# Turning Y block by block: sixteen copies from SBUF to SBUF per pair of tiles, in place of a store to DRAM and four loads

## The chip, the cores and the metric

One core of one Trainium2 chip runs the whole kernel. The metric is the device time of one execution in microseconds (us). The kernel before takes 1504.46 us, the median of three runs (1504.14 to 1504.58).

## What is computed

64 sequences (tiles) of 128 tokens with 512 channels pass one gated cross-attention layer and one gated feed-forward layer. Cut to what matters:

```python
x = x + tanh(g_xattn) * attention(layernorm(x), ctx)
#   attention: O = A V per head (A is one matrix per head, summed over the whole batch)
#   Y = (O - mean) / sqrt(var + eps) * gamma + beta       over the 512 channels of a token
#   out = (relu(xn @ wg) * Y) @ wo
x = x + tanh(g_ffn) * ffn(layernorm(x))
#   ffn: (silu(xn @ gate * gs) * (xn @ up * us)) @ down * ds,   512 -> 1408 -> 512
```

Every matrix product is made exact to about float32 by splitting operands in a high and a low part.

## The kernel before, in words

The 64 tiles are worked off in pairs, q = 0 to 31. The program of each of the five instruction streams is written out by hand, with semaphores between them. It has three stages. Up to about 380 us projections of all tiles are made and the relu gates W and the values V go to DRAM. From about 380 us to 1063 us the function `first_groups` runs eight groups of the feed-forward layer (each 11 steps of gate and up products and 4 steps of down products, 15 steps a group, four tiles each), and in the same steps the attention of pairs 2 to 31 is finished. After that six rounds do the feed-forward layer of the other 32 tiles with fewer products.

The attention of a pair is cut in pieces 0 to 12; `pieces(n)` lists for step n which piece of which pair is due. `first_step(q)` starts a new pair every 3.5 steps, in turns 3 and 4. A step is about 5 us, a pair about 20.7 us (620 us for thirty pairs). What each piece does for the turn of Y:

- Piece 1, ScalarE: `y_normal` writes the normalised tile, tokens on partitions, to `nbuf`.
- Piece 2, VectorE: `y_blocks` (line 1104) transposes each 32x32 block of both tiles in place of it, from `nbuf` to `tbuf` (in `misc`). The blocks are turned, but they do not yet stand where a full transpose would have them. For a tile from 6 on it first waits on `wys`, the store of the pair before, since `tbuf` is single.
- Piece 3, SyncE (SP): `y_out` stores `tbuf`, 512 KB, to `wy_scratch` in DRAM.
- Piece 4, SP: `y_in` waits for that store and for `wm` of the pair before (`wy_pair_mul`, line 1115, the last reader of `turned[0]`), and then loads through `blocks_in` (line 457) in four transfers of 128 KB, one for each 32 partitions of the target. They put the blocks in their places: channels on partitions.
- Piece 5, SP: `w_load` (line 364), 512 KB, the W of the same pair.
- Piece 6, ScalarE: `y_pair_affine` (line 713) waits for the four loads (`wyl`) and applies gamma and beta in place.
- Piece 7: `wy_pair_mul` on VectorE (needs the affine and W), `wy_pair_hi` on ScalarE (753), `wy_pair_lo` on GpSimd (1573); `x_again` on SP.
- Piece 9: `wo_pair` on TensorE (1803 and 1807); then x1 and its statistics on VectorE (1126 to 1132).
- Piece 12, SP: `x2_out` and `x1_store`. `x2_in` brings the normalised x1 back, turned in the same way by four loads, in steps 9 and 12 of a group.

All DMAs are issued by SP in one queue in the order of its program; a wait or a long issue holds all that stands behind it. TensorE works each step in one of two sets of PSUM banks: step n can start when VectorE has read step n-2 (`slot_free`; `hidden`, line 1267). The down products of steps 11 to 14 need the low parts that GpSimd makes (`hidden_lo`, line 1616) of all eleven hidden units; step 11 asks for the last one only near its end.

Of the kernel before, what the change touches and what calls it, by code (L numbers as in the profile page):

```python
# [52 lines left out]
def pieces(n):  # L53

    return [(q, n - first_step(q)) for q in range(2, B // 2) if 0 <= n - first_step(q) <= 12]
# [21 lines left out]
def gated_layer(nc, x, ctx_t, wh, wh_t, wg, wo, gate_t, up_t, down_t, cols, rows, decay, eye, out):  # L77
# [7 lines left out]
    with stack:  # L85
# [13 lines left out]
        def placed(name, shape, dt=f32):  # L99
            at[name] = -(-nc.sbuf_base // 32) * 32  # L100
            return sb(name, shape, dt)
# [12 lines left out]
        misc = placed("misc", [128, 1216])  # L114
        acc = misc[:, 0:512].rearrange("p (h n) -> p h n", h=4)
        stg = misc[:, 512:1216]
        tbuf = misc[:, 0:1024].rearrange("p (t n) -> p t n", t=2)
        wyt = [placed(f"wyt{i}", [128, 4, 256], f32r) for i in range(2)]
        turned = [placed(f"turned{i}", [128, 4, 256]) for i in range(2)]
        wh_first = [turned[0][:, 2 * i:2 * i + 2, :].rearrange("p k (h n) -> p (k h) n", h=2) for i in range(2)]  # L120
# [37 lines left out]
        nbuf = placed("nbuf", [128, 2, 512])  # L158
# [52 lines left out]
        wy_s = nc.dram_tensor("wy_scratch", [2, 128, D], f32, kind="Internal").ap()  # L211
# [90 lines left out]
        s = {name: stack.enter_context(nc.semaphore(f"s_{name}")) for name in SEMAPHORES}  # L302
# [4 lines left out]
        def _(e):  # L307
            p = Program(e, s)
# [34 lines left out]
            def v_load(q):  # L343
                if q:
                    p.wait_ge("vlo", q)
                else:
                    p.wait_ge("ctlo", ctl(NG - 1, 1))
                p.wait_ge("vst0", 16 * (q + 1))
                p.wait_ge("vst1", 16 * (q + 1))
                e.dma_start(raw[:, 0:2, :], v_s[:, 2 * q:2 * q + 2, :]).then_inc(s["vld"], 16)  # L350

            def w_load(q):
                if q == 0:
                    p.wait_ge("ctlo", ctl(NG - 1, 3))
                elif q == 1:
                    p.wait_ge("sst", 64)
                    p.wait_ge("sand", 16)
                elif q == 2:
                    p.wait_ge("tbwe", 2)
                else:  # L360
                    p.wait_ge("wylo", q - 2)
                p.wait_ge("wst0", 32 * (q // 2 + 1))
                p.wait_ge("wst1", 32 * (q // 2 + 1))
                e.dma_start(wt_of(q), w_s[q // 2, :, :, 256 * (q % 2):256 * (q % 2) + 256]).then_inc(s[f"wl{q % 2}"], 16)
# [12 lines left out]
            def x_again(q):  # L377
                if q >= 2:
                    p.wait_ge(f"x1s{q % 2}", 16 * (q // 2))
                else:  # L380
                    p.wait_ge("xn", 2 * q + 58)
                    if q:
                        p.wait_ge("ad", 1)
                e.dma_start(xr[:, 2 * (q % 2):2 * (q % 2) + 2, :], x_v[:, 2 * q:2 * q + 2, :]).then_inc(s[f"xa{q % 2}"], 16)

            def x1_store(q):
                p.wait_ge("x1", 2 * q + 2)
                e.dma_start(x1_s[:, 2 * q:2 * q + 2, :], xr[:, 2 * (q % 2):2 * (q % 2) + 2, :]).then_inc(s[f"x1s{q % 2}"], 16)

            def residual(q):  # L390
                p.wait_ge(f"x1s{q % 2}", 16 * (q // 2 + 1))
                if q >= 2:
                    p.wait_ge(f"out{q % 2}", 16 * (q // 2))
                else:
                    p.wait_ge("wolo", 4)
                    p.wait_ge("alo", 1)
                e.dma_start(xr[:, 4 + 2 * (q % 2):6 + 2 * (q % 2), :], x1_s[:, 2 * q:2 * q + 2, :]).then_inc(s[f"res{q % 2}"], 16)

            def out_store(q):
                p.wait_ge("of", 2 * q + 2)  # L400
                e.dma_start(out_v[:, 2 * q:2 * q + 2, :], xr[:, 4 + 2 * (q % 2):6 + 2 * (q % 2), :]).then_inc(s[f"out{q % 2}"], 16)

            def y_out(q):

                p.wait_ge("wyb", 2 * q - 2)
                if q > 2:
                    p.wait_ge("wyl", 64 * (q - 2))
                e.dma_start(wy_s.rearrange("t p n -> p t n"), tbuf).then_inc(s["wys"], 16)

            def x2_out(q):  # L410
                p.wait_ge("x2b", 2 * q - 2)
                e.dma_start(x2_s[q].rearrange("t p n -> p t n"), xbuf[:, :, :]).then_inc(s["x2s"], 16)
# [8 lines left out]
            def weights_copy(o, k):  # L421
                src, row = {G1: (gate_s, 0), G2: (gate_s, 256), U2: (up_s, 256)}[o]
                e.dma_start(ws_s[:, :, k, o, :].rearrange("j p n -> p j n"),
                            src[row + 128 * k:row + 128 * k + 128, :].rearrange("p (j n) -> p j n", n=128)).then_inc(s["gst"], 16)
# [27 lines left out]
            def blocks_in(scratch, dst, name):  # L452

                src = scratch.rearrange("t (u r) (c a j) -> a r c (t u) j", u=4, c=4, a=4)
                for a in range(4):
                    to = dst[32 * a:32 * a + 32, :, :].rearrange("r c (x j) -> r c x j", j=32)
                    e.dma_start(to, src[a]).then_inc(s[name], 16)

            def y_in(q):
                p.wait_ge("wys", 16 * (q - 1))  # L460
                p.wait_ge(*(("wm", q + 2) if q > 2 else ("wm", 4)))
                blocks_in(wy_s, turned[0], "wyl")

            def x2_in(q):
                p.wait_ge("x2s", 16 * (q - 1))
                if q > 2:
                    p.wait_ge("tb2e", q + 2)
                blocks_in(x2_s[q], turned[1], "x2l")
# [106 lines left out]
            for g in range(NS):  # L575
                for step in range(15):
                    if step == 0 and g:
                        out_store(2 * g - 1)
                    if step == 4:
                        residual(2 * g)  # L580
                        residual(2 * g + 1)
                    if 1 <= g <= 6 and step == 14:
                        weights_copy((G1, G2, U2)[(g - 1) // 2], (g - 1) % 2)
                    for q, piece in pieces(15 * g + step):
                        if piece == 12:
                            x2_out(q)
                            x1_store(q)
                        if piece == 3:
                            y_out(q)
                        if piece == 2 and 2 < q < B // 2 - 2:  # L590
                            v_load(q + 2)
                        if piece == 4:
                            y_in(q)
                        if piece == 5:
                            w_load(q)
                        if piece == 7:
                            x_again(q)
                    if g == 0 and step == 1:
                        x1_store(0)
                        x1_store(1)  # L600
                    if g == 0 and 2 <= step < 6:
                        down_load(step - 2)
                    if g + 1 < NS and step == (9 if g else 10):
                        x2_in(2 * g + 2)
                    if g + 1 < NS and step == (12 if g else 13):
                        x2_in(2 * g + 3)
                    if g == NS - 1:
                        if step == 5:
                            for q in range(4):
                                pair_in(2 * NS + q)  # L610
                        if step in (8, 9, 10):
                            weights_in(step - 8)
                    if step == 13:
                        out_store(2 * g)
# [3 lines left out]
            for m in range(NP):  # L618
                q = 2 * NS + 4 * m
                for j in range(NI):  # L620
                    n = NI * m + j
# [26 lines left out]
        def _(e):  # L648
            p = Program(e, s)
# [72 lines left out]
                affine(tile_of(turned[0], t), bank_y(t))  # L722

            def y_pair_affine(q):
                p.wait_ge("wyl", 64 * (q - 1))
                affine(turned[0], turned[0])

            def wy_hi(t):
# [139 lines left out]
            for g in range(1, NG):  # L868
                n, more = 4 * g + 4, g + 1 < NG
# [89 lines left out]
            for m in range(NP):  # L959
                for j in range(NI):  # L960
                    n = NI * m + j
# [19 lines left out]
        def _(e):  # L981
            p = Program(e, s)
# [114 lines left out]
            def y_blocks(t):  # L1097
                p.wait_ge("nr", t + 1)
                if t >= 6:
                    p.wait_ge("wys", 16 * (t // 2 - 2))  # L1100
                else:
                    p.wait_ge("alo", 1)
                    p.wait_ge("wolo", 4)
                e.transpose(tbuf[:, t % 2, :], nbuf[:, t % 2, :]).then_inc(s["wyb"])

            def wy_mul(t):
                p.wait_ge("aff", t + 1)
# [221 lines left out]
            for g in range(1, NG):  # L1329
                n, more = 4 * g + 4, g + 1 < NG  # L1330
# [117 lines left out]
            for g in range(NS):  # L1448
                for step in range(15):
# [15 lines left out]
                    for q, piece in pieces(15 * g + step):  # L1465
                        t = 2 * q
# [13 lines left out]
                    for q, piece in pieces(15 * g + step):  # L1480
                        t = 2 * q
# [7 lines left out]
            for m in range(NP):  # L1489
                t = 4 * NS + 8 * m  # L1490
# [3 lines left out]
                for j in range(NI):  # L1494
                    n = NI * m + j
# [646 lines left out]
```

## Time and profile before

| | |
|---|---|
| median of three runs | 1504.46 us |
| the profiled execution | 1504.5 us |
| its span, first to last instruction | 1502.7 us |
| TensorE busy in the span | 1482.3 us (99%) |
| VectorE, ScalarE, GpSimd busy | 1045.7, 679.0, 717.7 us |
| granted TensorE clock, mean of the span | 0.999 |
| mean busy share of 16 DMA engines by SP's queue | 67.4% |

The page gives each engine's busy time, the span in 40 slices, the DMA queues, the chain of work that ended last, and groups of instructions. PE is TensorE, PEld its weight loads, DVE VectorE, ACT ScalarE, POOL GpSimd, SP SyncE; "SPq L457" is a DMA issue at line 457. In a timeline a bracket gives how long the engine sat idle before the row and what ended that. SP has no compute work: its rows are issues, and their duration is the time for which the queue is held.

### The profile page before, as it was taken

The numbers are of one execution on the slowest core, as the hardware profiler recorded it, in microseconds if no ns is written. First come the engines' busy times: TensorE is split into PE (matmuls) and PEld (weight loads), VectorE is DVE, ScalarE is ACT, GpSimd is POOL, SyncE is SP. The second block draws the span as 40 slices with busy tenths as digits, with TensorE's granted clock in tenths as the row PEclk, the third lists the DMA queues.
The fourth block names the chain that finished last, engine by engine and source line by source line (L and its number), as shares of the span: only waits on it lengthen the run. The fifth ranks groups of instructions, "written<-read, shape, count | busy, mean of one in ns | idle before, by whom it ended". The sixth has DMA issues, their size and how long they took to land.

```text
span 1502.7 us, 20433 instructions
## 1 busy us (share of the span) xinstructions
PE 1482.3 (99%) x7226; PEld 1057.6 (70%) x7226; DVE 1045.7 (70%) x1516; ACT 679.0 (45%) x1067; POOL 717.7 (48%) x767
## 2 busy tenths in 40 slices
PE   7999999999999999999999999999999999999998
PEld 5888888888667777677677767666566666666665
DVE  7777778788657676767677676554767768768662
ACT  4444434445564545445354544534344344343442
POOL 5556666771444535435354544534137238137236
PEclk9999999999999999999999999999999999999999
DMA  6888888876688686777877787676383473572332
GB/s 231 295 267 272 267 273 281 260 223 227 209 247 242 175 255 206 206 243 210 228 233 204 224 220 234 181 222 158 101 223 114 117 216 114 138 211 95 130 109 85
DMA packets 374952, 306.09 MB, mean 204 GB/s; under 512 B 258560, under 2 KB 284672, under 8 KB 374656
## 3 DMA queue, kind: packets, MB, share of 16 engines
q1 hardware_dynamic: 374848, 304.74, 67.4%
q8 instruction: 60, 0.98, 0.3%
q14 instruction: 44, 0.36, 0.1%
HBM read 200.36 MB, written 117.31 MB: 211 GB/s over the span
## 4 chain that ended last, share of the span: by engine, by line
PE 87%; DVE 5%; POOL 3%; issue 2%; ACT 2%; DMA 1%; SPq 0%; DVEq 0%; POOLq 0%; ACTq 0%
PE ps L1815 15%; PE ps L1813 14%; PE pyb L1698 8%; PE ps L1733 5%; PE po L1698 5%; PE ps L1822 4%; PE ps L1820 4%; PE po L1815 4%; PE po L1813 4%; PE pyb L1803 3%; PE ptb L1803 3%; PE pyb L1822 3%; PE ptb L1822 3%; PE ptb L1820 3%; PE pyb L1820 3%; PE pyb L1807 2%
## 5 line engine op out<-in xcount | busy, mean ns | idle before, releaser
L1616 POOL TENSOR_TENSOR hid_low<-tmp,reg 128x512 f16<-128x512 f32 x88 | 118.7, 1349 | 132.4 <-ACT reg L764 132.4
L1698 PE MATMUL pyb<-reg,xreg 128*128 128x512 f32 x708 | 177.1, 397 | 2.0 <-DVE reg L1003 1.7
L1596 POOL TENSOR_TENSOR p5b<-p5b,p1b 128x512 f32<-128x512 f32 x44 | 56.5, 1283 | 215.5 <-ACT p5b L788 215.5
L1607 POOL TENSOR_TENSOR hsp<-hall,hsp 128x640 f16<-128x640 f32 (+2 forms) x72 | 136.3, 1909 | 33.2 <-ACT hsp L815 32.1
L1698 PEld LDWEIGHTS pyb<-reg,xreg 128*128 128x128 f32 x708 | 129.2, 188 | 28.6 <-DVE reg L1003 2.1
L834 ACT ACTIVATE tmp<-ps,colsb 128x512 f32<-128x512 f32 x88 | 60.5, 687 | 161.1 <-PE ps L1815 81.4
L1267 DVE SCALAR_TENSOR_TENSOR tmp<-ps,colsb,tmp 128x512 f32<-128x512 f32 x88 | 65.6, 746 | 78.2 <-PE ps L1813 43.0
L1573 POOL TENSOR_TENSOR wyt<-raw,wyt 128x1024 fp32r<-128x1024 f32 x30 | 73.8, 2461 | 83.6 <-ACT wyt L753 83.6
L1522 POOL TENSOR_SCALAR rs<-mv 128x1 f32<-128x1 f32 (+1 forms) x98 | 42.7, 436 | 138.8 <-DVE mv L991 106.7
L1815 PE MATMUL ps<-op,wbuf 128*128 128x512 f32 x352 | 103.9, 417 | 0.0
L1815 PE MATMUL ps<-reg,gate 128*128 128x512 f32 x352 | 103.3, 415 | 0.0
L1733 PE MATMUL ps<-reg 128*128 128x256 f32 x768 | 101.5, 285 | 0.8 <-DVE misc L1021 0.3
L1733 PEld LDWEIGHTS ps<-reg 128*128 128x128 f32 x768 | 97.1, 191 | 5.1 <-POOL reg L1569 1.4
L1527 POOL TENSOR_TENSOR rs<-rs,nhalf 128x1 f32<-128x1 f32 (+1 forms) x132 | 90.0, 682 | 11.0
L1815 PE MATMUL ps<-reg,up 128*128 128x512 f32 x352 | 91.9, 393 | 0.0
L1813 PE MATMUL ps<-op,wbuf 128*128 128x512 f16 x352 | 90.8, 380 | 0.3 <-issue 0.3
L1822 PE MATMUL ps<-xreg,reg 128*128 128x512 f32 x352 | 90.2, 403 | 0.8 <-POOL hid_low L1616 0.6
L1813 PE MATMUL ps<-x_low,gate 128*128 128x512 f16 x352 | 90.8, 380 | 0.0
L1234 DVE TENSOR_TENSOR nbuf<-po,p1b 128x512 f32<-128x512 f32 x44 | 30.4, 692 | 86.8 <-PE po L1813 43.6
L1813 PE MATMUL ps<-x_low,up 128*128 128x512 f16 x352 | 88.7, 380 | 0.8 <-DVE tmp L1267 0.7
L681 ACT ACTIVATE tmp<-pyb 128x512 f32<-128x512 f32 x59 | 35.3, 598 | 114.7 <-PE pyb L1698 114.6
L1569 POOL TENSOR_TENSOR reg<-raw,reg 128x512 fp32r<-128x512 f32 x62 | 83.2, 1341 | 5.0
(180 smaller groups left out, 3363.5 us busy)
## 6 DMA issues: line engine op xcount, KB each, us to landing
wbuf<-ws_scratch SPq DMA_DIRECT2D x44, 896.0 KB, 4.8
xr<-in_x SPq DMA_DIRECT2D x62, 512.0 KB, 5.6
raw<-in_ctx_t SPq DMA_DIRECT2D x32, 512.0 KB, 4.6
w_scratch<-tmp SPq DMA_DIRECT2D x64, 256.0 KB, 5.0
v_scratch<-tmp SPq DMA_DIRECT2D x64, 256.0 KB, 4.0
raw<-v_scratch SPq DMA_DIRECT2D x32, 512.0 KB, 6.7
x_scratch<-xr SPq DMA_DIRECT2D x32, 512.0 KB, 4.5
xr<-x_scratch SPq DMA_DIRECT2D x32, 512.0 KB, 5.9
```

The lines of the kernel that those rows point to most:

```text
L1527: e.tensor_tensor(dst, dst, nhalf[:, 0:dst.shape[-1]], ALU.pow).then_inc(s[name])
L1569: e.tensor_tensor(lo, raw[:, h, :], f(hi), ALU.subtract).then_inc(s["ctlo"])
L1573: e.tensor_tensor(wyt[1][:, :, :], wt_of(q), f(wyt[0][:, :, :]), ALU.subtract).then_inc(s["wylo"])
L1607: e.tensor_tensor(hsp[t % 2][1][:, i0:i1, :], hall[:, i0:i1, 128 * i:128 * i + 128], f(hsp[t % 2][0][:, i0:i1, :]), ALU.subtract).then_inc ...
L1616: e.tensor_tensor(hid[1][:, m % 11, :], tmp[:, m % 3, :], f(hid[0][:, m % 11, :]), ALU.subtract).then_inc(s["hlo"])
L1698: last = e.matmul(dst, lhs[a], rhs[b], start=(k == 0 and i == 0), stop=(k == n - 1 and i == 2))
L1733: last = e.matmul(ps[t % 2][:, h, :, :], ct[g % 2][i][:, h, 128 * b:128 * b + 128], wh_and_z(q, h, b), start=(n == 0), stop=(n == 2))
L1803: e.matmul(py(t), wyt_of(t)[0][:, k, :], wos[i][k], start=(k == 0 and i == 0), stop=False)
L1813: return e.matmul(dst, upper(wt), act[1], start=start, stop=stop, skip_group_check=True)
L1815: return e.matmul(dst, a, b, start=start, stop=stop, skip_group_check=True)
L1820: return e.matmul(dst, act, packed, start=start, stop=stop)
L1822: return e.matmul(dst, a, b, start=start, stop=stop)
```

## The change

`y_out` and `y_in` go, and `y_turn` stands at piece 4. It waits for the blocks (`wyb`) and for `wm` of the pair before, and issues sixteen transfers from `tbuf` straight to `turned[0]`: for each group a of 32 target partitions and each group u of 32 source partitions one transfer of 32 partitions x 8 blocks x 128 bytes, 32 KB. The semaphore `wyl` counts 256 for a pair. VectorE's `y_blocks` writes `tbuf` in another order within the partition (channel block outside, tile inside) and waits for the turn of the pair before (`wyl`), where it waited for that pair's store. The turn of x1 by way of DRAM stays as it is.

```diff
-        tbuf = misc[:, 0:1024].rearrange("p (t n) -> p t n", t=2)
+        tbuf = misc[:, 0:1024]
@@
-            def y_out(q):
+            def y_turn(q):
                 p.wait_ge("wyb", 2 * q - 2)
-                if q > 2:
-                    p.wait_ge("wyl", 64 * (q - 2))
-                e.dma_start(wy_s.rearrange("t p n -> p t n"), tbuf).then_inc(s["wys"], 16)
+                p.wait_ge(*(("wm", q + 2) if q > 2 else ("wm", 4)))
+                for a in range(4):
+                    to = turned[0][32 * a:32 * a + 32, :, :].rearrange("r c (t u j) -> r (c t) u j", u=4, j=32)
+                    for u in range(4):
+                        blocks = tbuf[32 * u:32 * u + 32, :].rearrange("r (x a j) -> r a x j", a=4, j=32)
+                        e.dma_start(to[:, :, u, :], blocks[:, a, :, :]).then_inc(s["wyl"], 16)
@@
-            def y_in(q):
-                p.wait_ge("wys", 16 * (q - 1))
-                p.wait_ge(*(("wm", q + 2) if q > 2 else ("wm", 4)))
-                blocks_in(wy_s, turned[0], "wyl")
@@
-                        if piece == 3:
-                            y_out(q)
...
                         if piece == 4:
-                            y_in(q)
+                            y_turn(q)
@@
             def y_pair_affine(q):
-                p.wait_ge("wyl", 64 * (q - 1))
+                p.wait_ge("wyl", 256 * (q - 1))
@@
             def y_blocks(t):
                 p.wait_ge("nr", t + 1)
                 if t >= 6:
-                    p.wait_ge("wys", 16 * (t // 2 - 2))
+                    p.wait_ge("wyl", 256 * (t // 2 - 2))
...
-                e.transpose(tbuf[:, t % 2, :], nbuf[:, t % 2, :]).then_inc(s["wyb"])
+                e.transpose(tbuf.rearrange("p (c t n) -> p c t n", c=4, t=2)[:, :, t % 2, :], nbuf[:, t % 2, :].rearrange("p (c n) -> p c n", c=4)).then_inc(s["wyb"])
```

## Rows read from the trace of the kernel before

**Rows 1.** The page: busy time, and the chain that ended last.
```profile
PE 1482.3 (99%) x7226; PEld 1057.6 (70%) x7226; DVE 1045.7 (70%) x1516; ACT 679.0 (45%) x1067; POOL 717.7 (48%) x767
PE 87%; DVE 5%; POOL 3%; issue 2%; ACT 2%; DMA 1%; SPq 0%; DVEq 0%; POOLq 0%; ACTq 0%
```

**Rows 2.** One stretch: length; PE, PEld, DVE, ACT, POOL busy; clock; DMA share.
```profile
380.00:1065.00 685.00, 681.75 (x3192) 474.08 (x3191) 452.40 (x661) 336.78 (x503) 306.42 (x360) 1.00 0.75 214
```

**Rows 3.** Waits of PE, 380 to 1065 us: total, times, longest.
```profile
PE ps L1820 <- POOL hid_low L1616: 0.6, 1, 0.6
...
PE pyb L1807 <- POOL wyt L1573: 0.2, 1, 0.2
```

**Rows 4.** Issues by source line: duration ns min/median/max; time to landing.
```profile
L457 SPq DMA_DIRECT2D turned<-wy_scratch x120: 557/674/2597, 390.8 to 986.2; - x120
...
DMA to landing us min/median/max: 2.6/3.3/7.9
...
L408 SPq DMA_DIRECT2D wy_scratch<-misc x30: 359/420/1222, 387.9 to 977.3; - x30
...
L364 SPq DMA_DIRECT2D raw<-w_scratch x31: 572/787/2092, 345.2 to 990.3; - x31
```

**Rows 5.** Timeline of SP, pairs 8 and 13: start, duration, line, transfer.
```profile
510.28 3.09 SPq L457 DMA_DIRECT2D turned<-wy_scratch  x4
513.42 0.66 SPq L412 DMA_DIRECT2D x_scratch<-xbuf  x1
...
514.70 0.79 SPq L364 DMA_DIRECT2D raw<-w_scratch  x1
...
608.92 3.15 SPq L457 DMA_DIRECT2D turned<-wy_scratch  x4
```

**Rows 6.** Timelines of DVE and ACT after pairs 8 and 13.
```profile
517.14 1.38 DVE L1104 STREAM_TRANSPOSE misc<-nbuf 128x512 f32<-128x512 f32 x2 [1.65 <-ACT nbuf L707]
521.37 2.07 ACT L713 ACTIVATE turned<-turned,colsb 128x256 f32<-128x256 f32 x4
523.47 1.23 DVE L1115 TENSOR_TENSOR raw<-raw,turned 128x1024 f32<-128x1024 f32 x1 [0.95 <-ACT turned L713]
...
619.41 1.29 DVE L1104 STREAM_TRANSPOSE misc<-nbuf 128x512 f32<-128x512 f32 x2
```

**Rows 7.** A hidden unit on DVE, and PE's next step in its banks.
```profile
500.56 0.75 DVE L1267 SCALAR_TENSOR_TENSOR tmp<-ps,colsb,tmp 128x512 f32<-128x512 f32 x1 [1.29 <-PE ps L1815]
...
505.29 1.04 PE L1813 MATMUL ps<-x_low,up 128*128 128x512 f16 x4
```

**Rows 8.** The chain that ended last, 405 to 432 us: start, length, what.
```profile
406.87 0.57 SPq L457
...
408.22 2.60 SPq L457
...
410.86 0.68 SPq L457
...
412.81 7.35 DMA raw<-w_scratch
...
428.76 1.19 PE pyb L1807 x4
```

**Rows 9.** Step 11 of the second group, 526 to 531 us.
```profile
526.80 0.75 DVE L1267 SCALAR_TENSOR_TENSOR tmp<-ps,colsb,tmp 128x512 f32<-128x512 f32 x1 [0.48 <-PE ps L1815]
...
529.52 1.27 POOL L1616 TENSOR_TENSOR hid_low<-tmp,reg 128x512 f16<-128x512 f32 x1 [3.69 <-ACT reg L764]
...
530.85 0.10 PEld L1820 LDWEIGHTS ps<-down_first,hid_low 128*128 128x128 f16 x1 [0.21 <-POOL hid_low L1616]
```

**Rows 10.** Waits of SP, 390 to 1010 us: total, times, longest.
```profile
SPq L40 <- DVE raw L1115: 163.1, 24, 13.6
...
SPq L457 <- DMA wy_scratch<-misc: 29.7, 11, 5.0
```

**Rows 11.** The page, W's load: count, KB each, median us to landing.
```profile
raw<-w_scratch SPq DMA_DIRECT2D x31, 512.0 KB, 6.2
```

## The prediction

> **What bounds the kernel now.** I read the page first: TensorE is busy for 1482.3 of 1502.7 us and the chain that ended last is 87% TensorE [rows 1]. The turn of Y takes place between 380 and 1065 us only, so I cut that stretch out: TensorE is busy in 681.75 of 685.00 us, idle for 3.25 us, at a granted clock of 1.00, the level of 2.4 GHz [rows 2]. This is the most that any relief of DMA, SP, VectorE or ScalarE can give back there; it is 0.22% of the time, and 0.2% (3.0 us) is about what a measurement of this kernel can tell from no change. The waits of TensorE in the stretch name no part of the turn directly; the nearest is 0.2 us for GpSimd's low part of W*Y, and the longest wait for the low part of a hidden unit is 0.6 us [rows 3]. So the question is not what is saved but whether the new order of SP's queue pushes something into TensorE's way. The DMA engines are busy for 0.75 of the stretch [rows 2], and SP often sits waiting: 163.1 us in 24 waits for the multiplication of the pair before, and 29.7 us in 11 waits for Y's own store [rows 10]. Of VectorE I need how late it may be: a hidden unit read by 501.31 (500.56 + 0.75) is asked for by TensorE at 505.29, a slack of 3.98 us [rows 7]. It is the tightest kind among the steady steps: there VectorE reads as soon as TensorE is done.
>
> **What is removed.** One store of 512 KB for each of thirty pairs: 0.42 us of SP's queue [rows 4], and the eleven waits of SP for it (29.7 us, [rows 10]). None of this is on TensorE's path: the loads start mostly when the multiplication of the pair before ends, not when the store lands. Credit: 0, at most the 3.25 us of idle TensorE.
>
> **What is added: issues.** Four issues of 128 KB become sixteen of 32 KB. The four take 557 ns at the least and 674 ns in the median each [rows 4], and 3.09 us together at pair 8 [rows 5]. No row shows a copy of 32 partitions x 8 runs from SBUF to SBUF. The store of Y (256 runs too, on 128 partitions) held SP for 359 ns at least, 420 in the median; W's load, with 512 runs, 572 [rows 4]. From one issue's end to the next start about 0.04 us pass (513.37 to 513.42 in [rows 5]). So a pitch of 0.40 us is the lower end (0.36 + 0.04) and 0.72 (0.674 + 0.04) the upper, if the count of runs should not matter at all. I take 0.45 (0.42 + 0.03, rounded), because 256 runs are what the store has. Sixteen are then 7.2 us (6.4 to 11.5) where four took 3.1. The bytes and the runs of 128 B are the same 4096 for a pair, so I cost the movement itself at no more than now and hidden below the issues. The last transfer should land some 2.3 us after its issue: the loads of 128 KB have a minimum of 2.6 and a median of 3.3 [rows 4], and these are a quarter of the size. From first issue to all landed: 15 x 0.45 + 2.3 = 9.0 us (8.2 to 14.1), where pair 8 has about 3.09 + 2.6 = 5.7 now.
>
> The Trainium skill speaks against this (DMA: Bandwidth & Descriptors, Rules for kernel authors: coalesce small transfers, below 64 KB one pays mostly overhead). Rows 5 show that overheads of neighbouring issues overlap here, four starting within 3.09 us though one lands 3.3 us after its issue [rows 4, 5]; if by the rule each of sixteen paid such a 2 us alone, a pair would need some 32 us, longer than the pair's 20.7, and the stage would be SP-bound.
>
> **What is added: a wait on VectorE.** `y_blocks` of the next pair waits until the turn has landed. At pair 8 the turn can start at 510.28 [rows 5] and the next blocks start at 517.14 [rows 6]: 6.86 us; every fourth pair from 8 to 28 is of this kind, by the list of pieces. 9.0 - 6.86 = 2.1 us of new wait there. Pair 13 stands for the roomy ones (608.92 to 619.41, 10.5 us) [rows 5, 6]; the rest lie between, so 0 to 2. Queued behind it are x1 with its statistics and the next hidden unit. The slack of 3.98 us [rows 7] hides 2.1. It costs something only where it falls ahead of step 11 of a group. Y's affine starts at 521.37 [rows 6], 11.09 us after the turn's start: 9.0 fits.
>
> **What is moved.** All behind the turn in SP's queue starts later by 7.2 - 3.1 = 4.1 us: x2_out, x1_store and w_load at pair 8. W's load is issued at 514.70 [rows 5]; at 518.8 plus a landing of 6.2 [rows 11] it is there at 525.0, and the multiplication that started at 523.47 [rows 6] is 1.5 us late. In most pairs the slack of this load hides the 4.1 us; pairs of the kind of 8 can lose 1 to 3 us on VectorE, again within 3.98.
>
> **Where it reaches TensorE.** Two places have no slack.
> (a) Pair 3, 406 to 429 us. The chain that ended last runs here through the four Y loads (406.87 to 411.54, 4.67 us, of which one issue stood for 2.60 us), W's load at 412.81 (7.35 us), and by way of GpSimd's low part to TensorE at 428.76 [rows 8]. The turn starts at the same moment (after the multiplication of pair 2) and holds the queue for 7.2 in place of 4.67 us: +2.5 us (1.8 to 6.8), all on the path. If the 2.60 us stand comes on top, it is 4.5.
> (b) Step 11 of the second group, right behind pair 8. The multiplication is 1.5 us late, so the hidden unit at 526.80 is about 1.5 late, and its low part at 529.52 too; TensorE already waited 0.21 us for it at 530.85 [rows 9]. +1.2 us. The 2.1 us of new wait ahead of the unit before it adds about 0.3.
> Sum: 2.5 + 1.2 + 0.3 = 4.0 us. In the other groups the multiplication of a pair of this kind falls two or more steps away from step 11, by the list of pieces, and TensorE's longest wait for a low part is 0.6 us [rows 3]; I take 0 for them.
>
> VectorE's transposes write four runs of 128 elements in place of one of 512; I cost this at nothing, up to 0.1 us each (60 of them, hidden by VectorE's idle third).
>
> **The sum.** 1504.5 us of the profiled execution (span 1502.7 and 1.8 around it; the median of the runs is 1504.46, the same) + 4.0 = 1508.5 us.
>
> **Rivals.**
> 1. Everything is absorbed. VectorE, ScalarE and SP idle enough, and at pair 3 the backlog of DMA is smaller because two stores are gone (the 2.60 us stand shows such a backlog [rows 8]), so that W lands when it did. For it: 3.25 us of idle TensorE in 685 [rows 2] show how forgiving the schedule is. Against it: the chain of rows 8 has not a microsecond of slack. Time 1504.5 (1503.5 to 1507). Chance 0.35.
> 2. Faster, the other side: the store and its traffic were behind part of the 3.25 us idle, and nothing new is late. It decides from the point where sixteen issues take no longer than the four plus the store, a pitch of 0.22 us, or where the queue's backlog ends sooner by more than the 2.5 us. At best 1501.3. Rows 4 hold no issue below 0.36. Chance 0.04.
> 3. The issue is dearer: a pitch of 0.6 to 0.72 us, since the four-issue rows stay at 0.67 however long the queue is free. The turn then needs 11 to 14 us, y_blocks waits 4.5 to 7 us in most pairs, which is over the slack of 3.98, and W comes 6.5 to 8.4 us late. At 0.72 some thirteen pairs lose 2.5 us on TensorE and pair 3 6.8: 1504.5 + 32 + 7 = 1543; at 0.6 mostly the ends of the groups and pair 3, about +15: 1520. Chance 0.13.
> 4. The page's rule, sixteen overheads one after another: 32 us for a pair instead of 20.7 gives 30 x 11.3 = +340 us. Chance 0.01.
>
> **How the numbers follow.** The forecast (1508.5, own range 1505.5 to 1513) has 0.47; about a sixth of it lies below 1507.5. Faster by over 0.2% 0.04; within 0.2% 0.35 + 0.08 = 0.43; slower 0.39 + 0.13 + 0.01 = 0.53. The range reaches down to 1503.8 for rival 1 and up to 1519 for the cheap end of rival 3: some 0.16 is left out.
>
> **What would show it.** Right: the turn's issues at about 0.41 us each, all sixteen within 7 to 7.5 us and landed in 9; a new wait of the transposes in `y_blocks` on a DMA into `turned`, about 2 us, 10 to 20 times, 30 to 45 us in total, with TensorE hardly idle; TensorE idle by 2 to 3 us more near 429 us behind GpSimd's `wyt`, and by about 1 near 531 us behind `hid_low`. SP's waits for the store gone. Wrong: if issues take 0.6 us or more (rival 3), if the transfers from SBUF land much later than 2.3 us after issue although the issues are short (ports or engines shared by both sides), or if TensorE's idle time in 380 to 1065 us stays at 3 us (rivals 1 and 2).

## The result and the profile after

The changed kernel takes 1598.66 us, the median of four runs (1596.0 to 1600.09), where the kernel before takes 1504.52 beside it: ratio 1.0626, 95% interval 1.0614 to 1.0639, so 94 us slower. The forecast said slower, by 4 us, within 1505.5 to 1513. The profiled execution spans 1596.7 us against 1502.7, 94.0 more.

The page of the changed kernel, the parts that answer rows 1, and the stretch of the turn (columns as in rows 2). The stage ends about 95 us later now, so a second stretch reaches to 1165 us:

```profile
PE 1509.0 (95%) x7226; PEld 1068.6 (67%) x7226; DVE 1045.9 (66%) x1516; ACT 679.8 (43%) x1067; POOL 715.2 (45%) x767
...
PE 50%; SPq 21%; DVE 12%; DMA 7%; issue 5%; ACT 3%; POOL 3%; DVEq 0%; ACTq 0%; POOLq 0%
SPq L411 17%; PE pyb L1694 8%; PE ps L1811 6%; PE ps L1809 6%; PE ps L1729 5%; PE po L1811 4%; PE po L1809 4%; DVE raw L1111 3%; PE pyb L1818 3%; PE ptb L1818 3%; PE ptb L1816 2%; PE pyb L1816 2%; PE po L1694 2%; DMA raw<-w_scratch 2%; DMA 
```
```profile
380.00:1065.00 685.00, 621.05 (x2817) 427.64 (x2816) 398.53 (x592) 304.17 (x456) 275.03 (x333) 0.97 0.59 168
380.00:1165.00 785.00, 713.46 (x3214) 486.87 (x3213) 456.69 (x668) 339.73 (x507) 306.01 (x361) 0.97 0.59 168
```

Every compute engine has the same work as before. But the chain that ended last, once 87% TensorE with nothing for SP's queue [rows 1], is half TensorE now, and 17% of it is line 411, the sixteen issues. TensorE was idle for 3.25 us of the stretch [rows 2]; now it is idle for 64 of 685. It is also busy for 26.7 us longer in all (1509.0 - 1482.3) with the same number of instructions, and the granted clock is 0.97 where it was 1.00. The other two stages have not changed. So of the 94 us, some 67 are new idle time of TensorE (94.0 - 26.7) and 27 are slower matmuls. TensorE waits for several engines; these are its two longest waits from 380 to 1165 us (total, times, longest), the first for VectorE to read a hidden unit, the second for the high part of W*Y:

```profile
PE ps L1809 <- DVE tmp L1263: 24.1, 12, 6.3
...
PE pyb L1799 <- ACT wyt L749: 15.4, 9, 4.1
```

The issues of the turn (columns as in rows 4) and who waited for them (us, times):

```profile
L411 SPq DMA_DIRECT2D turned<-misc x480: 585/611/2691, 387.6 to 1087.0; - x160
...
  DVE misc L1100: 163.7, 26
  ACT turned L709: 28.8, 11
...
DMA to landing us min/median/max: 1.9/1.9/6.4
```

An issue takes 611 ns, not 420. The turn spans 699.4 us from its first issue to its last (387.6 to 1087.0), where it spanned 595.4 [rows 4]: 104 us more, of which 8 are the longer last turn itself. The other 95 or so are 3.3 us for each of the 29 steps from pair to pair, so the loss is spread over the whole stage and not at a few places.

What a pair looks like, SP's timeline of the changed kernel (columns as in rows 5), pairs 9 to 11:

```profile
547.85 11.23 SPq L411 DMA_DIRECT2D turned<-misc  x16
559.12 0.60 SPq L415 DMA_DIRECT2D x_scratch<-xbuf  x1
559.76 0.47 SPq L388 DMA_DIRECT2D x_scratch<-xr  x1
560.27 0.85 SPq L364 DMA_DIRECT2D raw<-w_scratch  x1
...
576.07 10.91 SPq L411 DMA_DIRECT2D turned<-misc  x16
...
589.17 1.15 SPq L364 DMA_DIRECT2D raw<-w_scratch  x1
...
596.88 10.40 SPq L411 DMA_DIRECT2D turned<-misc  x16
```

An undisturbed turn, as that of pair 11, holds the queue for 10.40 us, and its last transfer lands 1.3 us after that, at 11.7 (the medians of the thirty turns are 10.79 and 12.17). Pair 8 shows how the delay comes back to its own start. These are rows of the chain that ended last between 495 and 553 us (start, length, what), from W's load for pair 6 to TensorE:

```profile
495.39 6.43 DMA raw<-w_scratch
501.92 2.05 DVE raw L1111
513.82 1.90 DMA turned<-misc
...
526.22 2.29 DVE raw L1111
538.37 1.89 DMA turned<-misc
540.99 0.67 DVE misc L1100
...
546.96 1.24 POOL hid_low L1612
548.34 4.61 PE ps L1818 x10
```

and VectorE, ScalarE and TensorE in the same stretch (in a timeline a bracket gives the idle time ahead of a row and what ended it):

```profile
540.35 1.31 DVE L1100 STREAM_TRANSPOSE misc<-nbuf 128x512 f32<-128x512 f32 x2 [6.54 <-DMA turned<-misc]
...
545.38 1.22 DVE L1111 TENSOR_TENSOR raw<-raw,turned 128x1024 f32<-128x1024 f32 x1
...
560.49 1.31 DVE L1100 STREAM_TRANSPOSE misc<-nbuf 128x512 f32<-128x512 f32 x2 [2.87 <-DMA turned<-misc]
...
574.82 1.18 DVE L1111 TENSOR_TENSOR raw<-raw,turned 128x1024 f32<-128x1024 f32 x1
...
560.42 2.08 ACT L709 ACTIVATE turned<-turned,colsb 128x256 f32<-128x256 f32 x4 [0.95 <-DMA turned<-misc]
...
548.34 4.61 PE L1818 MATMUL ps<-xreg,reg 128*128 128x512 f32 x10 [4.34 <-POOL hid_low L1612]
```

The multiplication of pair 7 ends at 528.51 (526.22 + 2.29). Only then may pair 8's turn start, and its last transfer lands at 540.3 (538.37 + 1.89). `y_blocks` of pair 9 has waited 6.54 us for that and starts at 540.35. Behind it on VectorE stand x1, the statistics, a hidden unit, and the multiplication of pair 8 (545.38 to 546.60). Only then may pair 9's turn start; it starts at 547.85, because SP is at other issues until 547.75. That is a loop: turn, landing, next pair's `y_blocks`, this pair's multiplication, next turn. It is tight in most pairs: `y_blocks` waits for the landing 26 times, and 25 of 29 turns start within 0.1 us of the end of the multiplication. The first round took 18.1 us (528.51 to 546.60), the next, in which more stands between `y_blocks` (560.49) and the multiplication (done at 576.00), 29.4. In the kernel before the same two rounds took 14.5 and 27.1 us (the multiplications end at 510.21, 524.70 and 551.77). The mean is now some 24 us a pair, where the period was 20.7.

### The profile page after: what moved, and what is told of

Same layout as the page of the kernel before. It is cut to its first block, busy times and chain, and to the rows that moved or that the text cites. A ratio compares the mean times of both kernels' runs of the same rounds, so it can differ in the third digit from the quotient of the medians.

```text
span 1596.7 us, 20734 instructions
## 1 busy us (share of the span) xinstructions
PE 1509.0 (95%) x7226; PEld 1068.6 (67%) x7226; DVE 1045.9 (66%) x1516; ACT 679.8 (43%) x1067; POOL 715.2 (45%) x767
## 4 chain that ended last, share of the span: by engine, by line
PE 50%; SPq 21%; DVE 12%; DMA 7%; issue 5%; ACT 3%; POOL 3%; DVEq 0%; ACTq 0%; POOLq 0%
SPq L411 17%; PE pyb L1694 8%; PE ps L1811 6%; PE ps L1809 6%; PE ps L1729 5%; PE po L1811 4%; PE po L1809 4%; DVE raw L1111 3%; PE pyb L1818 3%; PE ptb L1818 3%; PE ptb L1816 2%; PE pyb L1816 2%; PE po L1694 2%; DMA raw<-w_scratch 2%; DMA turned<-misc 2%
## 5 line engine op out<-in xcount | busy, mean ns | idle before, releaser
L1612 POOL TENSOR_TENSOR hid_low<-tmp,reg 128x512 f16<-128x512 f32 x88 | 113.6, 1292 | 109.7 <-ACT reg L760 109.7
L1100 DVE STREAM_TRANSPOSE misc<-nbuf 128x512 f32<-128x512 f32 x60 | 39.3, 692 | 166.3 <-DMA turned<-misc 163.7
L1520 POOL TENSOR_SCALAR rs<-mv 128x2 f32<-128x2 f32 (+1 forms) x34 | 8.2, 240 | 256.2 <-DVE mv L1128 256.1
L1818 PE MATMUL ps<-xreg,reg 128*128 128x512 f32 x352 | 96.3, 422 | 15.3 <-DVE tmp L1270 7.8
L760 ACT CAST reg<-tmp 128x512 fp32r<-128x512 f32 x88 | 54.1, 615 | 114.2 <-DVE tmp L1263 114.2
L1809 PE MATMUL ps<-x_low,gate 128*128 128x512 f16 x352 | 94.4, 392 | 1.5 <-DVE tmp L1263 1.5
L1818 PEld LDWEIGHTS ps<-xreg,reg 128*128 128x128 f32 x352 | 69.3, 199 | 34.1 <-DVE tmp L1270 8.9
```

The source lines that it names most:

```text
L1612: e.tensor_tensor(hid[1][:, m % 11, :], tmp[:, m % 3, :], f(hid[0][:, m % 11, :]), ALU.subtract).then_inc(s["hlo"])
L1809: return e.matmul(dst, upper(wt), act[1], start=start, stop=stop, skip_group_check=True)
L1818: return e.matmul(dst, a, b, start=start, stop=stop)
```

## The experiments

I name four theories. A: the loop just described, through the wait of `y_blocks`. B: SP's queue is held, whoever waits. C: transfers from SBUF to SBUF are slow in themselves, or disturb others. D: there are two loops, A's and a second through W's load, which stands behind the sixteen issues and which the multiplication needs before the next turn may start; both must be broken. Each kernel is the changed one with the edit shown, unless the text says otherwise.

**Four transfers in place of sixteen, from SBUF to SBUF.** 128 KB each. The blocks don't go to their places, since the source is read in another pattern.

```diff
-                    for u in range(4):
-                        ... e.dma_start(to[:, :, u, :], blocks[:, a, :, :])
+                    runs = misc[32 * a:32 * a + 32, :].rearrange("r (x j) -> r x j", j=38)
+                    e.dma_start(to, runs[:, :, 0:32]).then_inc(s["wyl"], 16)
```

> The changed kernel with four transfers of 128 KB from SBUF to SBUF a pair, each of 32 partitions x 32 runs of 128 bytes, from the same partitions as its target; the blocks do not come to their right places, all bytes, runs and waits are those of the change. A and B alike (the number of issues is the cause): the four hold SP for about 3 us, land within 5 to 6, and the time is that of the kernel before or a little less, 1502 to 1507 us. C: the time stays near 1590 us.

Measured 1505.68 us, ratio 1.0011 (1.0002 to 1.0021). With the same bytes, the same runs of 128 B, the same wait in `y_blocks` and no store, the kernel is within 2 us of the one before. The four do not come cheap one by one: an issue takes 748 ns in the median, a turn holds SP for 3.65 us and has landed after 7.1, not 5 to 6. Still C falls: with the same bytes copied from SBUF to SBUF, 92 of the 94 us are gone. (They stay within their own partitions; so do those of "full width" below, which are sixteen and slow.) Saving the store and its landing brings nothing either, as the forecast had it.

**Twelve of the sixteen transfers.** A quarter of the turn is left out.

```diff
-                    for u in range(4):
+                    for u in range(3):
```

> The changed kernel with twelve of the sixteen transfers of a pair (the source group u = 3 is left out, so a quarter of the blocks of turned Y keeps old data). In the changed kernel an issue takes 0.65 us from start to start, the sixteen hold SP for 10.4 us and have landed 11.7 us after the first. Twelve should hold 7.8 and land after 9.1 us: nearly the 7.2 and 9.0 that the prediction took. Theory A (a wait on VectorE longer than its slack of 4 us): the wait of y_blocks falls from about 6.5 to 2 to 4 us and most of the loss is gone: 1508 to 1522 us. Theory B (SP's queue held, so W and the turned x1 come late, each microsecond costing in proportion): three quarters of the hold beyond the four loads' 3.1 us is 4.7 of 7.3, so 1504 + 94 x 4.7/7.3 = 1565 us. Theory C (copies from SBUF to SBUF are slow or disturb others): proportional to bytes, about 1575 us.

Measured 1528.0 us, ratio 1.0153 (1.0136 to 1.0170): 24 us lost, where an even share of 94 would be 63 (8 of the 12 added issues) to 71. B's 1565 and C's 1575 us are far off. A's range ended at 1522, 6 us below, so A comes nearest, but the loss is more than it allowed.

**Before, with Y's four loads cut in sixteen.** The kernel before, its store kept, its source in DRAM, its wait in `y_blocks` on the store; only each load of 128 KB is cut in four of 32 KB.

```diff
-                blocks_in(wy_s, turned[0], "wyl")
+                src = wy_s.rearrange("t (u r) (c a j) -> a u r c t j", u=4, c=4, a=4)
+                for a in range(4):
+                    for u in range(4):
+                        e.dma_start(to[:, :, :, u, :], src[a, u]).then_inc(s["wyl"], 16)
```

> The kernel before, with Y's four loads of 128 KB from DRAM cut in sixteen of 32 KB (same bytes, same runs, the store kept; tbuf is free again as soon as the store has landed). SP is held for about 10.4 us a pair as in the change, but y_blocks on VectorE waits for the store alone. A: the loss is mostly gone, 1506 to 1525 us, since only W, the turned x1 and Y's affine are late. B: as slow as the change, 1580 to 1600 us. C: 1504 us.

Measured 1623.03 us, ratio 1.0793 (1.0775 to 1.0811). Worse than the change itself, without SBUF as source and without the new wait, and above all three ranges. So the number of issues is enough to cause such a loss. The issues of the turn, and the longest waits of VectorE and of TensorE in 380 to 1190 us and one of SP (total, times, longest):

```profile
L466 SPq DMA_DIRECT2D turned<-wy_scratch x480: 557/617/1566, 391.1 to 1105.4; - x160
```
```profile
DVE raw L1119 <- DMA raw<-w_scratch: 94.5, 20, 14.1
...
PE pyb L1807 <- ACT wyt L757: 52.2, 17, 5.4
...
SPq L466 <- DMA wy_scratch<-misc: 56.8, 19, 5.7
```

`y_blocks` waits for no DMA here. But W's load comes late for the multiplication in 20 pairs, and the affine waits for the turn in 20 (72.1 us). So A alone falls: a loss of this size needs no wait in `y_blocks`. SP also waits longer for Y's own store (56.8 us, where it was 29.7 [rows 10]); that may be why this kernel is slower than the change, and was not tested apart.

**`y_blocks` one piece later.**

```diff
-                        if piece == 2:
+                        if piece == 3:
                             y_blocks(t)
```

> The changed kernel with y_blocks at piece 3 in place of 2 on VectorE, one step (some 5 us) later; nothing else moved, all sixteen transfers stay. A: of the wait of 6.5 us a pair 4 to 6 go, 1508 to 1530 us. B: the queue is held as long as before, 1585 to 1600 us. C: the same as B.

Measured 1569.26 us, ratio 1.0434 (1.0405 to 1.0463), between A and B. The longest wait of VectorE for a DMA:

```profile
DVE raw L1111 <- DMA raw<-w_scratch: 66.6, 16, 13.3
```

The wait of `y_blocks` falls from 163.7 us in 26 to 19.0 in 8, and the wait for W rises from 17.4 in 6 to 66.6 in 16. The one loop is broken and the other takes its place, which gave D.

**W's load amid the turn.**

```diff
                 for a in range(4):
+                    if a == 2:
+                        w_load(q)
...
-                        if piece == 5:
-                            w_load(q)
```

> The changed kernel with W's load issued between the eighth and the ninth transfer of the same pair's turn, not behind the sixteenth and what follows it. Theory D: two loops close from pair to pair, each as long as a pair's period of 20.7 us or longer: V, through VectorE (multiplication, turn landed after 11.7, y_blocks of the next pair, 8 to 13 us of work queued behind it, next multiplication: 20 to 24.5), and W (multiplication, 10.4 of issues, x2_out and x1_store, W's load 5 to 7, next multiplication: 19 to 22). This breaks W alone; V stays and is the longer one: 1575 to 1598 us. If the hold of SP's queue as such sets the time, nothing changes: 1598 or, by the interruption of 0.8 us, 1605.

Measured 1602.63 us, ratio 1.0654 (1.0636 to 1.0672). That is in the range of the theory of the hold, not in D's: to break only W's loop does nothing while the other still runs.

**Both together.**

> The changed kernel with both: y_blocks at piece 3 and W's load amid the turn. All sixteen issues stay and hold SP for 11.2 us. Theory D: both loops are broken, 1508 to 1530 us, clearly less than y_blocks at piece 3 alone (1569). If the hold as such sets the time: 1565 to 1600 us.

Measured 1549.52 us, ratio 1.0303 (1.0286 to 1.0321): half of the 94 us is back. It lies between the two ranges, 20 us above D's. What is left, in the waits of DVE, ACT and PE from 380 to 1150 us:

```profile
DVE raw L1111 <- ACT turned L709: 34.8, 11, 8.5
...
ACT reg L754 <- DMA turned<-x_scratch: 48.5, 11, 11.2
...
PE ps L1811 <- DVE x_low L1151: 7.6, 2, 3.9
```

The affine waits for the turn itself, and the next group's x (`turned<-x_scratch`), which stands in the same queue, comes late too. So there are more than two ways from the held queue to TensorE, and D as stated is only half shown: breaking its two loops brings half of the loss back. Worked out from the timelines, with the short gaps between neighbours counted in, SP is occupied by issues for 17.2 us of each pair's 21.9, where it was 10.9 of 20.4 before; so what stands in its queue is often late.

**Eight issues by SP, eight by ScalarE**, in piece 4 behind the affine of its list (`y_turn_rest` issues a = 2 and 3, with the waits of `y_turn`):

```diff
-                for a in range(4):
+                for a in range(2):
...
+                        if piece == 4:
+                            y_turn_rest(q)
```

> The changed kernel with eight of the sixteen issues (targets 64 to 127) moved from SP to ScalarE's queue, at the end of the step of piece 4. Each queue is held for 5.2 us, the turn has landed about 7 to 8 us after its start. Theory D: both loops fall to 16 to 19 us, under the period: 1504 to 1515 us, if ScalarE, idle for half its time, bears 5.2 us a pair; if it does not, its silu comes late and the time is 1520 to 1560 us. If it is the transfers and not their issue that cost, 1590 us.

Measured 1613.22 us, ratio 1.0726 (1.0708 to 1.0744). Waits of ScalarE and of TensorE:

```profile
ACT reg L770 <- DVE tmp L1276: 114.5, 26, 14.6
ACT reg L770 <- issue: 92.5, 20, 6.9
...
PE ps L1822 <- DVE tmp L1276: 41.5, 7, 9.9
```

SP is relieved (5.2 us of hold), but the eight issues, with their wait for the multiplication, stand in ScalarE's stream among its work for the hidden units; I put the row with "issue" down to them. TensorE then waits up to 9.9 us for a bank. None of the given ranges held. This edit does not test D; it shows the price of an issuing engine that has compute work of its own.

**Eleven and fourteen transfers**, for the curve (`min(4, 11 - 4 * a)` and 14; the rest of the turn is left out).

> The changed kernel with eleven of the sixteen transfers of a pair (five are left out, so those blocks of turned Y keep old data). Eleven issues hold SP for 11 x 0.65 = 7.15 us, the 7.2 that the prediction took for sixteen. Law of the closed loop, from the three runs so far (hold 7.8, 10.0, 10.4 us and 24, 82, 94 us of loss): free up to about 7.0 us, then each microsecond of hold costs each of some 29 pairs one: 1504.4 + 29 x 0.15 = 1508.7 us, between 1505 and 1516. If on the other hand the prediction's way from hold to time was wrong as well as the price of an issue, the time is far from 1508: 1520 us or more.

> The changed kernel with fourteen of the sixteen transfers (two left out, their blocks keep old data): hold 9.1 us. Law of the closed loop: 1504.4 + 29 x 2.1 = 1565 us (1555 to 1575). If the loss came in a jump, once a step of TensorE is missed, it would be near that of twelve (1528) or of sixteen (1598) and not between.

Measured 1519.6 (1.0100, 1.0083 to 1.0116) and 1563.57 us (1.0391, 1.0371 to 1.0411). Fourteen came out as expected, eleven 4 us above its range. With the others, by the medians of the thirty turns (worked out from the starts, ends and landings of their issues):

| transfers | hold, us | landed, us | time, us | over before | per us of hold since the row above |
|---|---|---|---|---|---|
| four, from DRAM (before) | 2.98 | 5.3 | 1504.4 | | |
| four, from SBUF | 3.65 | 7.1 | 1505.7 | 2 | |
| eleven | 7.15 | 8.5 | 1519.6 | 15 | 4 |
| twelve | 7.80 | 9.2 | 1528.0 | 24 | 14 |
| fourteen | 9.41 | 11.0 | 1563.6 | 59 | 22 |
| sixteen | 10.79 | 12.2 | 1598.7 | 94 | 26 |

Undisturbed turns hold 7.14, 7.79, 9.10 and 10.40 us for eleven to sixteen and have landed after 8.45, 9.09, 10.40 and 11.70; by these the last two steps cost 27 us for each us of hold. Between 3.65 and 7.15 us no run tells where the loss begins. From about 7.8 us on, every us of hold costs 22 to 27 us, nearly one for each of the thirty pairs, which is what a loop does that is tight in most of its rounds. With twelve the loss is not spread like this: set against the kernel before, instruction for instruction, TensorE falls behind by 4 us up to 550 us, by nothing from there to 750, and by 20 after that.

**What sets 0.6 us?** Three kernels with sixteen issues each; the blocks don't go to their places in any, and the last leaves out seven eighths of the turn.

```diff
+ one run:    e.dma_start(turned[0][32*a:32*a+32, u, :], tbuf[32*u:32*u+32, 256*a:256*a+256])
+ full width: e.dma_start(turned[0][:, i//4, 64*(i%4):64*(i%4)+64], tbuf[:, 64*i:64*i+64])
+ tiny:       e.dma_start(to[:, 0:1, u, :], blocks[:, a, 0:1, :])
```

> The changed kernel with sixteen transfers of 32 KB whose 32 partitions have one contiguous run of 1024 bytes each in place of eight of 128 (blocks go to wrong places; bytes, number of issues, partitions and waits are those of the change). If the shape of the access pattern sets what an issue costs, it takes 0.37 to 0.45 us from start to start (the trace has 0.36 for the transfers of one contiguous run per partition), the sixteen hold SP for 6 to 7 us and have landed after 8: less than the twelve of the first experiment, so 1504 to 1515 us. If an issue costs 0.65 us whatever its shape, the time is that of the change, 1590 to 1600 us.

> The changed kernel with sixteen transfers of 32 KB over all 128 partitions, one run of 256 bytes each (blocks go to wrong places; bytes, count of issues and waits are those of the change). If it is the 32 partitions of a transfer that make its issue take 0.6 us, these take 0.32 to 0.42 us as the 128-partition transfers of the kernel do, the hold is 6 to 7 us, and the time 1503 to 1508 us. If a copy with SBUF on both sides costs 0.6 us to issue whatever its shape, the hold stays at 10 us and the time near 1586 us.

> Of each of the sixteen transfers only the first of its eight blocks is copied (32 partitions x one run of 128 bytes, 4 KB; seven eighths of the turn are left out). Issue theory (an issue in a series costs about 0.6 us whatever it moves): duration 0.55 to 0.62 us, sixteen hold the queue for 9 to 10 us, and by the runs with fourteen (9.1 us, 1563) and sixteen (10.1 us, 1587) the time is 1560 to 1587. Size theory (the price follows the bytes or runs that are moved): about 0.42 us each as for single issues, hold 6.7 to 7.2, time 1505 to 1520, as with eleven transfers.

The issues of the three in this order (duration min/median/max, ns):

```profile
L409 SPq DMA_DIRECT2D turned<-misc x480: 507/591/2492, 388.6 to 1073.2; - x160
```
```profile
L409 SPq DMA_DIRECT2D turned<-misc x480: 465/601/2425, 387.8 to 1074.4; - x160
```
```profile
L411 SPq DMA_DIRECT2D turned<-misc x480: 508/591/2466, 387.9 to 1070.3; - x160
```

Times 1585.86 us (1.0545, 1.0526 to 1.0564), 1587.46 (1.0554, 1.0536 to 1.0571) and 1582.69 (1.0522, 1.0504 to 1.0539). One run of 1 KB for each of 32 partitions, 256 B for each of 128 partitions, or 128 B for each of 32: always 591 to 601 ns, against 611 for the change's eight runs. Shape, width and even size (4 KB or 32 KB) account for 20 ns. Only the first issue of a series is cheaper: in the medians by place in the series it is 530, 482 and 530 ns, and the second is at 592 to 602 already; in the change itself the first takes 603. The theory that the shape is dear falls, the issue theory holds. Why the second and all later ones take 0.6 us is open; no run looked behind the issue. Two rows limit the finding: the issues of 128 KB took more (674 ns from DRAM, 748 from SBUF), and the store of x1 takes 0.47 us at 559.76 above, though it follows seventeen others at 0.04 us. So standing behind another issue does not by itself make one cost 0.6 us.

## Why the prediction was wrong

**What bounds the kernel, and the credit of 0.** Right. Four transfers without the store take 1505.68 us: nothing was to be had.

**The pitch of an issue: the step that failed first.** I took 0.45 us, because the store of Y has 256 runs and took 420 ns [rows 4]. That store stands alone in the queue. The row to take was the load's own, 674 ns in a series of four, which I had as the upper end: it was the nearer row, and the number of runs, by which I chose, turned out to count for 20 ns. Measured: 611 ns, pitch 0.65, hold 10.4 us instead of 7.2. (A slip beside it: by its own terms the landing ranged from 8.3 to 13.1 us, not 8.2 to 14.1.) The rows gave this pitch as rival 3 (0.6 to 0.72), with a chance of 0.13; the argument in it, that the four stay at 0.67 however long the queue is free, was the better one.

**Movement hidden below the issues, the landing of 2.3 us.** Right; 1.9 us. The DMA share fell from 0.75 to 0.59. Sixteen landed in 11.7 us (15 x 0.65 + 1.9), where I had 9.0.

**Transposes that write four runs at nothing.** Right: 692 ns in the mean on the page of the changed kernel, where they took 707 before.

```profile
L1100 DVE STREAM_TRANSPOSE misc<-nbuf 128x512 f32<-128x512 f32 x60 | 39.3, 692 | 166.3 <-DMA turned<-misc 163.7
```

**The wait on VectorE.** Forecast: about 2 us, 10 to 20 times, 30 to 45 us in all. Measured: 163.7 us in 26 waits, up to 10.9 us. The wait is where it was foretold (the row above), and its cause too. At pair 9 it is 6.54 us, well over the 3.98 of slack. I had also misread how early it comes: I took pair 8's 6.86 us from the start of a turn to the next `y_blocks` for the shortest. The trace of the kernel before has six pairs below 5 us, the shortest pair 23 with 1.76 us (the same view as in rows 5 and 6):

```profile
822.76 3.26 SPq L457 DMA_DIRECT2D turned<-wy_scratch  x4
824.52 1.38 DVE L1104 STREAM_TRANSPOSE misc<-nbuf 128x512 f32<-128x512 f32 x2 [0.28 <-ACT nbuf L707]
```

**The sum by pairs: the step that failed second.** I held each pair's delay against a slack on its own, counted two places (+4.0 us), and put all others at 0. The run with eleven transfers tells this apart from the price of the issue: its hold is 7.14 us, almost exactly my 7.2, it lands even sooner (8.45 against 9.0), and it loses 15 us, not 4. Its waits of VectorE and TensorE:

```profile
839.79 1.30 DVE L1100 STREAM_TRANSPOSE misc<-nbuf 128x512 f32<-128x512 f32 x2 [6.51 <-DMA turned<-misc]
...
844.96 1.14 PE L1809 MATMUL ps<-x_low,up 128*128 128x512 f16 x4 [1.93 <-DVE tmp L1263]
...
470.66 1.20 PE L1811 MATMUL ps<-reg,up 128*128 128x512 f32 x4 [2.20 <-DVE x_low L1151]
```

Pair 3 costs 2.0 us of idle TensorE there and step 11 of the second group 0.4, much as forecast. But TensorE is idle for about 17 of the 705 us from 380 to 1085, where it was 3.25 before, so most of it lies where I had put 0. The first two rows are the pair with the shortest distance: `y_blocks` of pair 24 waits 6.51 us, over the slack. The third is a path that the forecast did not have at all: x1's turned loads (line 460) stand behind the sixteen in the same queue, and through ScalarE's cast and VectorE's `x_low` they reach TensorE. And as the hold grows, a late `y_blocks` makes the multiplication late, and the multiplication releases the next turn, so a delay is passed on to the next pair and the slack is not there twice. So the 90 us of error are some 11 by the response to the hold as I had forecast it, and 79 by the dearer issue together with the loop that it closes; rival 3 had the right pitch of 0.6 to 0.72 but not the loop, and still gave only about 15 us over before at 0.6 and 39 at 0.72.

**What is moved, and the affine.** At pair 8 all behind the turn comes 7.3 us later (10.40 against 3.09), not 4.1, and that puts W's load into a loop of its own, turn to W to multiplication to turn, which the forecast had as a single late multiplication. The affine does not fit any more: 11.7 us are over its 11.09, and it waits for the turn 11 times, 28.8 us in all. Right: SP's waits for the store are gone, and its wait for the multiplication of the pair before [rows 10] has shrunk, because the queue is late itself:

```profile
SPq L40 <- DVE raw L1111: 116.1, 25, 10.0
```

**Pair 3, +2.5 us.** Right in place, short in size. TensorE there (columns as in rows 8's timeline), where it waited 0.21 us before:

```profile
430.47 3.65 PE L1799 MATMUL pyb<-reg,wyt 128*128 128x512 f32 x8 [3.90 <-ACT wyt L749]
```

It waits 3.90 us, and the eight matmuls take 3.65 us. What ends the wait is ScalarE's high part of W*Y, not the low part by GpSimd that I had named; both follow from the same multiplication.

**Step 11 of the second group, +1.5 us.** Right in place: it is the row at 548.34 above, with a wait of 4.34 us for the low part of a hidden unit. In the kernel before these ten matmuls start at 526.53, so TensorE was already 17.5 us behind before this wait (548.34 - 4.34 - 526.53).

**Rival 4, sixteen overheads one after another.** Wrong in this form: the landings overlap, 1.9 us each and all sixteen in 11.7. Yet four transfers with the same bytes take 1505.68 us and sixteen 1598.66. The Trainium skill's advice to coalesce small transfers (DMA: Bandwidth & Descriptors, Rules for kernel authors) is borne out by this pair of runs; what it saves here is the issue's time on SP.

**What was missing altogether: the clock.** After its new waits TensorE runs at the lower of its two levels for a while. The timeline of before has the same ten matmuls at line 1822, then the windows of the changed kernel around 548 us (columns as in rows 2):

```profile
526.53 2.43 PE L1822 MATMUL ps<-xreg,reg 128*128 128x512 f32 x10
```
```profile
542.00:545.00 3.00, 1.99 (x9) 1.05 (x7) 2.86 (x7) 0.36 (x1) 0.09 (x1) 1.00 1.03 341
545.00:549.00 4.00, 0.66 (x2) 0.60 (x3) 3.81 (x7) 3.50 (x5) 2.94 (x5) 0.68 1.10 222
549.00:553.00 4.00, 4.00 (x11) 2.72 (x10) 1.47 (x2) 2.50 (x4) 2.37 (x2) 0.50 0.69 175
553.00:557.00 4.00, 4.00 (x18) 2.44 (x17) 3.97 (x5) 0.00 (x0) 3.92 (x3) 0.96 0.31 51
```

The granted clock falls from 1.00 to 0.50 (2.4 to 1.2 GHz) during the wait of 4.34 us and is back at 1.00 before 557. The ten matmuls take 4.61 us in place of 2.43: the wait of 4.34 us costs 2.2 more. The eight at pair 3 take 3.65 us, where eight of the same kind take 2.20 at 512.24 in the kernel before. Over the stretch to 1165 us a mean clock of 0.97 is, by an estimate, (1 - 0.97) x 2 x 785 = some 47 us at the lower level, and half of that is lost, in line with the 26.7 us of longer busy time. The forecast had priced a TensorE wait at its own length.

## What to carry to other kernels

Count the DMA instructions in a series, not only their bytes or runs, and price each by a row that stands in a series of its kind: here 0.65 us of the issuing queue each. List all that stands behind the series in the same queue, and look for the pair with the least room, not a typical one. Then look who releases the series: if its own consequence does (landing, a transpose, a product, the next turn), add up the whole loop round by round; where it is tight, each us is paid again in nearly every round. A wait of the busiest engine costs its length and what the clock gives back late.

## What the runs showed of the hardware

- In a series of sixteen, an issue by SP takes 591 to 617 ns in the median, whether it moves 4 or 32 KB, on 32 or 128 partitions, in 32 to 256 runs, from SBUF or DRAM; the first of a series 482 to 603. In a series of four with 128 KB each it takes 674 ns from DRAM and 748 from SBUF.
- A copy of 32 KB from SBUF to SBUF lands 1.8 to 1.9 us after its issue, one of 4 KB after 1.7, one of 128 KB after 3.8, and 32 KB from DRAM after 2.2. The landings overlap: sixteen have landed 11.7 us after the first issue.
- The granted clock of TensorE fell to 0.50 during a wait of 4.34 us and was back at 1.00 within 9 us of its end; the ten matmuls behind it took 2.2 us more.
- With eight issues of each turn given to ScalarE, its casts for the hidden units started 92.5 us late in 20 waits for which the profile names no other engine, and the kernel took 1613 us against 1599.
